# AdaLN ternary FFN on one core: seven inner products inside P2 and P5, and an earlier mix

## The reference

```
def _bitlinear(x, w):
    scale = jnp.mean(jnp.abs(w))
    q = jnp.round(jnp.clip(w / (scale + EPS), -1.0, 1.0))
    return x @ (q * scale).T
gate = _bitlinear(y, w_gate); up = _bitlinear(y, w_up)
out = x + _bitlinear(gate * up, w_down)
```

## Time and profile before

| | |
|---|---|
| median of 3 runs | 1728.03 us (1727.51 to 1728.21) |
| profiled execution, span | 1726.1 us (first to last instruction; no other time of that execution is shown) |
| TensorE busy | 1707.7 us, 99% |
| VectorE busy | 1096.0 us, 63% |
| ScalarE busy | 575.6 us, 33% |
| GpSimd busy | 28.0 us, 2% |
| chunk 3, first product to first product of chunk 4 | 205.42 us |

### The profile page before, as it was taken

How to read it: one execution, slowest core, us unless ns; L and a number is a source line. 1 busy time by engine, 2 the same in 40 slices (tenths; PEclk the granted TensorE clock), 3 DMA queues, 4 the chain that set the end, 5 groups by cost and what they waited for, 6 DMA issues and landing times.

```text
span 1726.1 us, 31355 instructions
## 1 busy us (share of the span) xinstructions
PE 1707.7 (99%) x12424; PEld 1215.6 (70%) x12424; DVE 1096.0 (63%) x1786; ACT 575.6 (33%) x921; POOL 28.0 (2%) x59
## 2 busy tenths in 40 slices
PE   6999999999999999999999999999999999999999
PEld 5554545968769596795958768596776959678684
DVE  6898895555766468554685646755576545855464
ACT  6887732312333133230333213231233313323120
POOL 0010000000000000000000000000000000000000
PEclk9999999999999999999999999999999999999999
DMA  8666626312242032420224211331223313132021
GB/s 342 249 229 239 221 96 219 121 44 97 76 148 96 22 108 77 168 66 22 107 102 164 65 75 54 129 137 43 97 76 126 101 40 108 65 124 79 29 87 49
DMA packets 59735, 194.06 MB, mean 112 GB/s; under 512 B 5280, under 2 KB 5600, under 8 KB 59584
## 3 DMA queue, kind: packets, MB, share of 16 engines
q1 hardware_dynamic: 56432, 177.49, 28.9%
q0 software_dynamic: 2560, 14.36, 2.2%
q10 hardware_dynamic: 592, 0.09, 0.0%
HBM read 160.90 MB, written 31.01 MB: 111 GB/s over the span
## 4 chain that ended last, share of the span: by engine, by line
PE 97%; DVE 2%; DMA 1%; issue 0%; ACT 0%; SPq 0%; DVEq 0%
PE ps L881 52%; PE ps L938 25%; PE ps L658 17%; PE ps L899 2%; PE ps L761 1%; DMA xa<-in_x_dram 1%; DVE wsum L1318 0%; DVE ys L1413 0%; DVE msk L1458 0%; DVE ys L1380 0%; DVE xa L1529 0%; DVE prod L1496 0%; DVE yp L1418 0%; ACT wdT L1106 0%; SPq L493 0%
## 5 line engine op out<-in xcount | busy, mean ns | idle before, releaser
L881 PE MATMUL ps<-yp,wgT 128*128 128x256 f16 x4116 | 902.4, 273 | 1.1 <-issue 1.1
L881 PE MATMUL ps<-wuT,wgT 128*128 128x256 f16 x4116 | 902.4, 273 | 0.0
L881 PEld LDWEIGHTS ps<-yp,wgT 128*128 128x128 fp8e4 x4116 | 402.9, 98 | 50.8 <-issue 2.9
L881 PEld LDWEIGHTS ps<-wuT,wgT 128*128 128x128 fp8e4 x4116 | 402.7, 98 | 48.3
L938 PE MATMUL ps<-wdT,inter 128*128 128x512 fp8e4 x1960 | 433.2, 379 | 0.0
L938 PEld LDWEIGHTS ps<-wdT,inter 128*128 128x128 f16 x1960 | 191.1, 98 | 227.2 <-issue 1.4
L1762 DVE SCALAR_TENSOR_TENSOR xr<-ps,osc,xr 128x512 f32<-128x512 f32 x210 | 156.4, 748 | 168.2 <-PE ps L938 128.4
L1711 DVE TENSOR_TENSOR wdT<-ps,msk 128x512 f32<-128x512 f32 (+1 forms) x77 | 51.3, 666 | 207.1 <-PE ps L881 207.1
L1241 ACT COPY raw<-ps 128x512 f32<-128x512 f32 (+1 forms) x77 | 43.7, 567 | 314.6 <-PE ps L881 314.0
L1248 ACT COPY msk<-ps 128x512 f32<-128x512 f32 (+1 forms) x77 | 43.6, 567 | 138.1 <-PE ps L881 138.1
L1263 ACT COPY inter<-ps 128x256 f32<-128x256 f32 x70 | 26.1, 372 | 180.1 <-PE ps L881 180.1
(11 more groups left out here) (229 smaller groups left out, 1497.9 us busy)
## 6 DMA issues: line engine op xcount, KB each, us to landing
wgT<-wcomb SPq DMA_DIRECT2D x70, 896.0 KB, 4.7
wdT<-dcomb SPq DMA_DIRECT2D x14, 2240.0 KB, 10.9
xa<-in_x_dram SPq DMA_DIRECT2D x8, 2048.0 KB, 7.8
out_dram<-xr SPq DMA_DIRECT2D x64, 256.0 KB, 2.0
wcomb<-xa POOLq DMA_DIRECT2D x17, 448.0 KB, 3.0
xr<-in_L_ffn_w_down_dram SPq DMA_DIRECT2D x9, 512.0 KB, 5.5
inter<-in_L_ffn_w_gate_dram SPq DMA_DIRECT2D x7, 512.0 KB, 16.6
wdT<-in_L_ffn_w_up_dram SPq DMA_DIRECT2D x7, 512.0 KB, 4.4
```

Source lines behind the costliest of these rows:

```text
L881: last = nc.tensor.matmul(out, w, operand(i, OPERAND[what])[:, k, :], start=(start and h + k + i == 0), stop=(k == KQ - 1 and i == 1), ski ...
```

## The change

In chunks 3 to 8 (`inners` is empty for `c == FIRST`) P2 (pairs 0 to 9) and P5 (pairs 1 to 9) are themselves computed by seven products of half size in each direction: 2 contraction tiles x gate or up or a difference x 128 tokens. Their weight differences (four blocks per product and pair) are made by GpSimd in chunk 2, stored in DRAM (`wsub`) and loaded 128 KB at a time into two slots. The sums of the operands (`inner_sums`, `inner_lo`, `hi_inner`) are made beside group 1. All partial sums of both products share bank ps5 (`IB`, `lowers`) and a buffer in SBUF (`p2`, `uppers`); ScalarE copies them into the target bank (`inner1` to `inner3`), VectorE adds (`inner_upper`), and TensorE accumulates the last three onto that. `c11` and `i11` of a pair move behind `c12`, `i12` and `sum4` of the pair before; in pairs 0 and 1 `residual` moves behind `copy_p16`. Pairs 2 to 5 mix two slices each, `norms` moves to step 1 of down group 0, `scales` behind its step 2 and `scale_y` to its steps 3 to 10. The space of `aT` is taken over, so that it is stored once in DRAM (`aggd`) and SP loads the diagonal blocks from there, ahead of x. `down_load(1)` is issued two pairs later.

```
# TensorE, pairs(c, more)
+    mix = [2 * (p - 2) + i for i in range(2) if more and p - 2 in range(KH // 2)]
     product(c, p, "P1")
+    if inners(c, p):
+        inner_a(c, p)
+        if p: product(c, p - 1, "P4")
+        else: product(c, p, "P5", 0)
+        inner_b(c, p)
+        for k in mix[0:1]: conv(c + 1, k)
+        product(c, p, "P6", 0)
+        inner_g(c, p)
+        product(c, p, "P6", 1)
+        if plain5: product(c, p, "P5", None if p else 1)
+        for k in mix[1:2]: conv(c + 1, k)
+        if p: product(c, p - 1, "P3")
+        inner_d(c, p)
+        product(c, p, "P7")
+        continue
+def inner(what, p, out, x, w, start=False):
+    for k in range(2):
+        for i in range(2):
+            wk = (blocks_s(sub_ring[...][p % 2])[:, w, k, :] if isinstance(w, int)
+                  else ring(p, w[0], BLOCK[what], 2 * w[1] + k))
+            last = nc.tensor.matmul(out, wk, inner_x(what, i, x)[:, k, :], ...)
+def inner_a(c, p):        # waits for the loads, c11 of p-1, c12 of p-2
+    for q, what in enumerate(inners(c, p)):
+        inner(what, p, lowers[:, q, 0], IA11, (0, 0), q == 0)
+        last = inner(what, p, lowers[:, q, 1], IS1, 0)
+def inner_b(c, p):        # waits for inner1;  IS2, difference 1, onto lowers[:, q, 0]
+def inner_g(c, p):        # waits for inner2;  IS3, difference 2, onto lowers[:, q, 0]
+def inner_d(c, p):        # waits for inner_upper
+    for what in inners(c, p):
+        inner(what, p, bank[:, 0:TH], IA12, (0, 1))
+        inner(what, p, bank[:, 2 * TH:3 * TH], IS4, (1, 1))
+        inner(what, p, bank[:, TH:2 * TH], IA22, 3).then_inc(s_done[what], 1)
# ScalarE
+def inner1(c, p): for q, what ...: copy(bank[:, 0:TH], lowers[:, q, 0])
+def inner2(c, p): copy(uppers[:, 0:n, 0, :], lowers[:, 0:n, 0, :])
+def inner3(c, p): copy(uppers[:, 0:n, 1, :], lowers[:, 0:n, 0, :])
+                  for q, what ...: copy(bank[:, TH:2 * TH], lowers[:, q, 0])
     copy_p1(c, p)
+    if inners(c, p): inner1(c, p)
-    if p < 2:
+    elif p < 2:
         residual(c, 2 * p); residual(c, 2 * p + 1)
     if p: gate21(c, p - 1)
+    if inners(c, p): inner2(c, p); inner3(c, p)
     copy_p16(c, p)
+    if inners(c, p) and p < 2:
+        residual(c, 2 * p); residual(c, 2 * p + 1)
# VectorE
+def inner_upper(c, p):
+    for q, what in enumerate(inners(c, p)):
+        V.tensor_tensor(bank[:, HALF:TOK], uppers[:, q], lowers[:, q, 1] broadcast to both, ALU.add)
# SP
 def next_x(c):
     sp.wait_ge(s_xr, NT * c)
     sp.wait_ge(s_y, KH * c + KH)
+    for h in range(2):
+        sp.dma_start(ablk[h * C:(h + 1) * C, :, h * C:(h + 1) * C],
+                     aggd[h * C:(h + 1) * C, bass.ds((c + 1) * NT, NT), :]).then_inc(s_abd, 16)
     load_x(c + 1)
# GpSimd, once, in chunk 2
+for p in range(NPR):
+    for q, what in enumerate(INNER):
+        (four tensor_tensor subtractions of 128x256 fp8, each waiting for the one before)
+        nc.gpsimd.dma_start(wsub[p, q], sub_stage[q][p % 2])
```

More of the change, by code:

```diff
@@ L116, in adaln_ternary_ffn @@
     OUT = {"P1": (0, 0), "P2": (0, 0), "P6": (0, 1), "P3": (0, 1), "P4": (2, 0), "P7": (2, 1), "P5": (2, 1), "D": (2, 1)}
+    INNER, TH = ('P2', 'P5'), P
+    NI = len(INNER)
+    IA11, IA12, IS1, IS2, IS3, IS4, IA22 = range(7)
     BLOCK = {"P1": 0, "P6": 1, "P5": 2, "P2": 3, "P7": 4, "P4": 5, "P3": 6}
@@ L372, in wd_block, with blocks_s, inners, inner_x @@
             return wd_flat[:, at:at + BLK]
+        IB, isums = ps[5], sums.rearrange("p (s k n) -> p s k n", s=4, k=2)
+        uppers = p2[:, :].rearrange("p (q a n) -> p q a n", q=2, a=2)
+        lowers = IB[:, :].rearrange("p (q b n) -> p q b n", q=2, b=2)
+        a_flat = aT[:, :, :].rearrange("p t c -> p (t c)")
+        sub_hl = [[a_flat[:, (2 * q + i) * TOK:(2 * q + i + 1) * TOK].bitcast(f16)
+                   .rearrange("p (s k n) -> p s k n", s=4, k=2) for i in range(2)] for q in range(2)]
+        sub_ring = ([hi_r[:, :].bitcast(f32), sub1[:, :].bitcast(f32)], [g_r[:, i * HALF:(i + 1) * HALF] for i in range(2)])
+        sub_stage = [[a_flat[:, (4 + 2 * q + i) * HALF:(5 + 2 * q + i) * HALF] for i in range(2)] for q in range(2)]
+        def blocks_s(b):
+            return b.bitcast(f8).rearrange("p (s k n) -> p s k n", s=4, k=2)
+        def inners(c, p):
+            if isinstance(c, int) and c == FIRST or p == NPR:
+                return ()
+            return INNER[0:1 if p == 0 else NI]
+        def inner_x(what, i, s):
+            if s in (IA11, IA12, IA22):
+                k, t = {IA11: (0, 0), IA12: (2, 0), IA22: (2, TH)}[s]
+                return operand(i, OPERAND[what])[:, k:k + 2, t:t + TH]
+            return sub_hl[INNER.index(what)][i][:, s - IS1]
+        def inner_bank(p, what):
+            return PA if what == "P2" else PC[p % 2]
         psb = [p[:, :].bitcast(bf16) for p in ps]
@@ L831, in down, with product @@
                 last.then_inc(s_dn, 1)
-            def product(c, p, what):
+            def product(c, p, what, half=None):
                 n = NS * (c - FIRST) + p
@@ L872, in product @@
                     pe.wait_ge(s_c22, n + 1)
-                if p == 0:
+                if p == 0 and half != 1:
                     pe.wait_ge(s_ylo, KH * c + OPERAND[what] + 1)
-                waited(c)
-                for h in range(2 if p < NPR else 1):
+                if half != 1:
+                    waited(c)
+                for h in range(2 if p < NPR else 1) if half is None else (half,):
                     out = bank[:, h * HALF:(h + 1) * HALF]
@@ L883, in product @@
                                                     skip_group_check=True)
-                last.then_inc(s_done[what], 1)
+                if half != 0:
+                    last.then_inc(s_done[what], 1)
+            def inner(what, p, out, x, w, start=False):
+                for k in range(2):
+                    for i in range(2):
+                        wk = (blocks_s(sub_ring[INNER.index(what)][p % 2])[:, w, k, :] if isinstance(w, int)
+                              else ring(p, w[0], BLOCK[what], 2 * w[1] + k))
+                        last = nc.tensor.matmul(out, wk, inner_x(what, i, x)[:, k, :], start=(start and k + i == 0),
+                                                stop=(k + i == 2), skip_group_check=True)
+                return last
@@ new lines, in inner_b @@
+            def inner_b(c, p):
+                pe.wait_ge(s_e1, NPR * (c - FIRST - 1) + p + 1)
+                waited(c)
+                for q, what in enumerate(inners(c, p)):
+                    last = inner(what, p, lowers[:, q, 0], IS2, 1)
+                last.then_inc(s_ib, 1)
+            def inner_g(c, p):
+                pe.wait_ge(s_e2, NPR * (c - FIRST - 1) + p + 1)
+                waited(c)
+                for q, what in enumerate(inners(c, p)):
+                    last = inner(what, p, lowers[:, q, 0], IS3, 2)
+                last.then_inc(s_ig, 1)
@@ L943, in down_group @@
                     last.then_inc(s_dn, 1)
+                    if more and not g and d == 1:
+                        norms(c + 1)
                     if more and g and d == 4:
@@ L998, in pairs @@
                         product(c, p - 1, "P4")
-                    if more and p - 2 in range(KH):
-                        conv(c + 1, p - 2)
+                    for k in mix[0:1]:
+                        conv(c + 1, k)
                     product(c, p, "P6")
                     product(c, p, "P5")
+                    for k in mix[1:2]:
+                        conv(c + 1, k)
                     if p:
@@ L1209, in hi_quarters @@
                 for s in range(8):
+                    if s == S4:
+                        hi_inner(c, 0)
                     hi_quarter(c, s)
+                for q in range(1, NI):
+                    hi_inner(c, q)
             first = 2 * NPR + 1
@@ L1724, in sums3 @@
                 dve.wait_ge(s_i21, NS * (c - FIRST) + p + 1)
+                if p == 0 and later(c):
+                    dve.wait_ge(s_ilo, NI * (c - FIRST))
                 if p or later(c):
@@ L1794, in tail @@
                         for what, k in steps[d]:
-                            if what == "scale":
-                                scale_y(c + 1, k)
+                            if what == "inner":
+                                inner_sums(c + 1, k)
+                            elif what == "lower":
+                                inner_lo(c + 1, k)
                             elif what == "sum":
@@ L1816, in pairs @@
                     if p == GRP + 1:
+                        if more:
+                            add_l1(c + 1, KH - 1)
                         for d in range(len(DOWN[0])):
                             output2(c, 0, d)
-                    if p < NPR:
+                            if more and d == 2:
+                                scales(c + 1)
+                            if more and d - 3 in range(KH):
+                                scale_y(c + 1, d - 3)
```

(10 more changed lines are left out.)

203 lines of the change are left out of this document (177 added, 26 removed).

## The result

The kernel after takes 1733.99 us, median of seven runs (1730.92 to 1736.6); the kernel before, run beside it, 1727.68 (1727.51 to 1729.76). The ratio is 1.0035 [1.0026, 1.0045]: slower by 0.35%, where 1720.6 and faster were forecast. The profiled execution took 1732.3 with a span of 1730.3, 4.2 us more than the span of before, and a mean granted clock of 0.995. In the seven runs time and clock go together: 1730.92 at 0.995, 1733.99 at 0.992, 1736.6 at 0.990.

The account below looks back on a forecast made before the run. TensorE was taken as the bound, busy 1707.7 of 1726.1 us. The median 1728.0, less 20.4 for the inner products, plus 13.0 for the late x, gave 1720.6 us; its own range was 1716 to 1728, the whole range 1708 to 1738.

Parts of the forecast that it names:

- Inner products: P2 and P5 in chunks 3 to 8: 114 products each save 0.179 us, 20.4 us gained, at 56 ns a small matmul.
- Handoffs: TensorE to ScalarE and VectorE inside a pair: cost nothing, tightest room 0.25 us; if uncovered, 0.1 to 0.5 us a pair.
- The rest at nothing: Mix slices, norms, scaling, last down group and GpSimd's weight differences: no cost.
- The late x: First mix slice in chunks 3 to 7: TensorE waits 2.6 us for the x load, 13 us lost in all.
- The way of TensorE: From the end of P6 in pair 1 to the mix slice: four products and 48 small matmuls, 9.68 us.
- ScalarE's terms: From the end of P6 in pair 1: 0.20 us to start, copy 0.48, x copies and the queue's wake 2.29.
- One issue to the next is 0.61, 1.22 together: DMA queue: the two diagonal-block DMAs issued ahead of x delay its issue by 1.22 us.
- Then 7.7 to land: The x load lands 7.7 us after issue; 0.3 us was added for the small pieces ahead of it.
- Granted clock 1.00 throughout: TensorE's clock stays at full speed despite the waits, so the sum held no clock cost.
- Rival 2: Each wait for x in five chunks also pulls the clock down, 1.7 us each: 8.5 us, 1729 us; chance 0.16.
- Rival 1: Before the mix slice x is not late, or some 2 us are hidden: full gain, 1708 us; chance 0.12.
- Rival 3: Small matmuls in the 24-matmul piece cannot be fed: 84 ns each, 69 us lost, about 1803 us; chance 0.12.

Follow-up runs that it names:

- e1: The changed kernel with all four copies of x into xr in pair 0 and none in pair 1: 1708.64 us, ratio 0.9887 to before.
- e4: The changed kernel without the inner products (P2 and P5 plain, differences not loaded), the rest of the change kept: 1728.42 us, ratio 1.0001 to before.
- e7: The changed kernel with the copies of x right behind the first inner copy in pairs 0 and 1: 1714.1 us, ratio 0.992 to before.
- e5: The kernel before with only the x copies of pairs 0 and 1 moved behind copy_p16 in chunks 3 to 8: 1730.2 us, ratio 1.0012.
- e6: The changed kernel with all x copies in pair 0 and only P2 by inner products, P5 plain: 1718.13 us, ratio 0.9942 to before.
- e3: The changed kernel with 32 overwritten matmuls of 256 columns before the first mix slice in chunks 3 to 7: 1726.35 us, ratio 0.9989 to before.
- e2: The changed kernel with x issued ahead of the two DMAs of the diagonal blocks: 1724.12 us, ratio 0.9987 to before.

## Why the prediction was wrong, point by point

- **Inner products: right.** 20.4 us forecast, 19.8 measured (e1 against e4). The 98 ns "in every case" for a load was read too widely (it holds for fp8, f16 and bf16; f32 loads are recorded with 173 to 333 in before), but nothing hung on it. The 24 small matmuls of the last piece start 56 ns apart, at the end of the run as at its start; in one such piece of after, in a plain pair of chunk 3, the first starts at 617.41 and the 24th at 618.69, 23 steps of 55.7 ns:

```profile
617.41 0.22 PE L983 MATMUL ps<-yp,wgT 128*128 128x128 f16 x1
617.47 0.22 PE L983 MATMUL ps<-wuT,wgT 128*128 128x128 f16 x1
...
618.64 0.22 PE L983 MATMUL ps<-yp,g_r 128*128 128x128 f16 x1
618.69 0.22 PE L983 MATMUL ps<-wuT,g_r 128*128 128x128 f16 x1
```

- **Handoffs: right**, no wait in after; e7 shows how thin they are. VectorE's adds into PSUM took 426 ns (the second row below; 0.42 taken) and ScalarE's PSUM to PSUM copies 0.26 (0.27 taken, the line).
- **The rest at nothing: right** (e4: +0.1 us). GpSimd is busy for 89.3 us where it was 28.0 and holds nobody up; chunk 2, first product to first product, takes 205.3 us where it took 205.1.
- **The late x: the mechanism was right, its size wrong.** Forecast 2.6 us in five chunks, 13 in all; measured 3.6 in chunk 3 and 17.6 in all (16.9 in the first row below, less 0.2 of a wait in chunk 1, plus 0.17 five times). The way of TensorE (9.68) and ScalarE's terms held. Two terms failed. "One issue to the next is 0.61, 1.22 together": it was 1.64, the row priced an issue behind a load of x, and the two new ones are apart by 0.8 each (why, no run tells).

  "Then 7.7 to land", with 0.3 for small pieces: it was 8.54 in chunk 3, and 8.44 in the mean of chunks 3 to 7. Means of the same five chunks in the other kernels: without small pieces 7.7 (before) and 7.6 (e5); with them ahead and the next ring load 4 us or more behind, 7.9 (e4, e1) and 8.0 (e6); with them ahead and that load 1.1 to 2.0 us behind, 8.4 (after), 8.2 (e3) and 8.5 (e7). So the small pieces come to 0.2 to 0.4, near what I had added, and the ring load and the loads of the differences close behind to 0.2 to 0.6 more (the ring load alone cost nothing in e5). This is a reading of means and no more: with the very same spacing e7 has 7.9 and 8.0 in two chunks and 8.8 to 8.9 in three, and what decides between them is open.

  1.64 - 1.22 = 0.42 and 8.54 - 8.0 = 0.54 make 3.6 of the 2.6. The upper end of the stated wait, 4.1, stands on no term: by the prediction's own worst case for the small pieces, 4 us beyond the head start, it would be over 6. The waits of TensorE put down to x in after, then the group of VectorE's adds into PSUM:

```profile
PE ps L742 <- DMA xa<-in_x_dram: 16.9, 6, 3.8
```
```profile
L1943 DVE TENSOR_TENSOR ps<-p,ps 128x256 f32<-128x256 f32 x114 | 43.6, 426 | 56.7 <-ACT ps L1469 56.7
```
- **The clock: the step that turned the sign.** "Granted clock 1.00 throughout" was wrong: the sum put the cost of the clock at nothing. Rival 2, given 0.16, was right in place and price: four falls in the profiled run for 6.6 us, 7.6 us by e3, 8.5 worked out. With the measured waits alone the change would still have come out 2 us faster (1725.8); the clock alone, on top of the forecast waits, would have made 1728.8, the time of before within 1 us. The loss of 6 us needs both. I gave it little because the earlier trace rows hold a stretch without a fall too. But in that stretch TensorE was busy for 0.56 of 3 us; the row nearest to a whole wait of 2.6 us was the idle time of 2.03 us, and a fall had followed it.
- The sum with the measured sizes: 1728.0 - 19.8 + 17.6 + 7.6 = 1733.4, measured 1733.99.
- Rival 1 (no wait), 1708, is what e1 reached once x was moved: 1708.64. Rival 3 fell: 24 small matmuls in a row start 56 ns apart, and not 84.

## What to carry to other kernels

When TensorE is the bound and idles nowhere, a move that makes its input late can cost twice: the wait, and the slow clock behind it. So price a new wait of the lengths seen here (2 to 4 us) with up to 1.7 us more, and look first for a place where the buffer comes free sooner (here the copies of x in the pair with the least work for ScalarE, worth 25 us). A landing time read from one row is one draw: the same 2 MB took 7.5 to 8.9 us here, up to 1 us apart in one kernel with the same neighbours. And two DMAs whose issue I took at 0.61 each held the queue for 0.82 each.

## What the hardware showed that was not expected

- Idle times of TensorE in the two kernels that wait, and whether the granted clock fell to 0.50 there: 3.45, 3.18, 3.83, 2.97 fell, 3.32 did not (after); 2.79 and 2.19 fell, 2.09, 1.91 and 1.76 did not (e2). Longer ones fall more often, but 3.32 without a fall beside 2.19 with one shows that length alone does not decide. What else does is open.
- The slowest run of after (1736.6, mean clock 0.990) is 4.3 us above the profiled one (1732.3, 0.995), which had four of five possible falls. One fall more is worth 1.7 us, so the rest comes from elsewhere: a longer low clock near the start, as in the table, is one candidate, longer waits another. Which it was is not shown, as only one execution of each kernel is traced.
- The two DMAs of the diagonal blocks, 512 pieces of 256 bytes in all, land in 2.5 to 2.9 us ahead of x (median of the two, in every chunk of every kernel that has them) and in 6.9 to 7.9 behind it (e2).
- The Trainium skill's "TensorE: Matmul & The Clock Gate", section Back-to-back issue gap, gives about 81 ns for a sustained stream of loads and matmuls at N=128. The trace does not agree: 56 ns over 24 in a row, the figure of its formula for an isolated gap.
